# A windowed attention block with routed regions: x and the output with channels on partitions, and one reciprocal that also spreads its result

## The reference

```
xc  = group_norm(x)                                    # per image and group of 8 channels
q, k, v = split(xc @ qkv_w.T + qkv_b)                  # 256 channels each
q_r, k_r = mean of q, k over each of 7 x 7 regions     # a region is 8 x 8 positions
idx = top_k(q_r @ k_r.T, 4)                            # four regions for every region
# for every region and each of 8 heads of 32 channels:
attn = softmax((q * 256**-0.5) @ k[idx].T)             # 64 queries, 4 * 64 = 256 keys
o    = attn @ v[idx]
lepe = depthwise_conv3x3(v, lepe_w) + lepe_b
out  = x + ((o + lepe) @ out_w.T + out_b)
```

## Time and profile before

| | |
|---|---|
| median of 3 runs | 1920.2 us (1920.08 to 1926.36) |
| the profiled execution, first to last instruction | 1916.1 us |
| PE busy | 1767.0 us, 92% |
| DVE busy | 1613.2 us, 84% |
| ACT busy | 1587.6 us, 83% |
| POOL busy | 694.3 us, 36% |
| granted TensorE clock, mean | 0.990 |

### The profile page before, as it was taken

One profiled execution on the slowest core, in us unless ns is written; L12 is line 12 of the kernel. 1 busy time (PEld: TensorE's weight loads), 2 busy tenths in 40 slices (PEclk: granted clock), 3 DMA queues, 4 the chain that ended last, 5 costly groups with the idle time before them and its releaser, 6 DMA issues.

```text
span 1916.1 us, 75037 instructions
## 1 busy us (share of the span) xinstructions
PE 1767.0 (92%) x25560; PEld 1163.4 (61%) x25560; DVE 1613.2 (84%) x3819; ACT 1587.6 (83%) x5017; POOL 694.3 (36%) x2060
## 2 busy tenths in 40 slices
PE   6968999999999999999999999999999999977776
PEld 4535666666666666666666666666666666654444
DVE  4788998889998999898898899988988888876554
ACT  3648989899988999898898899888998888877775
POOL 1013433433433343434344334433433333333332
PEclk9989999999999999999999999999999999999999
DMA  4313444334443444344443344434443333333332
GB/s 114 85 48 99 113 132 113 114 112 135 118 122 99 132 119 123 110 120 117 124 115 113 109 130 118 119 109 125 116 121 97 109 97 111 103 106 90 93 101 89
DMA packets 163286, 211.71 MB, mean 110 GB/s; under 512 B 17760, under 2 KB 143840, under 8 KB 162912
## 3 DMA queue, kind: packets, MB, share of 16 engines
q1 hardware_dynamic: 141408, 129.84, 24.0%
q0 software_dynamic: 21504, 77.08, 13.3%
HBM read 155.46 MB, written 51.38 MB: 108 GB/s over the span
## 4 chain that ended last, share of the span: by engine, by line
SPq 51%; PE 25%; issue 9%; DVE 8%; DMA 5%; ACT 2%; POOL 0%; POOLq 0%; ACTq 0%; DVEq 0%
SPq L279 38%; SPq L254 11%; PE chunk_bank L818 8%; PE pt_bank L906 5%; PE s_bank L893 3%; DVE lepe L573 3%; PE o_bank L920 3%; DMA v_sel<-v_dram 3%; PE chunk_bank L836 3%; SPq L269 2%; DVE neg_max L669 1%; DMA v_dram<-v_stage 1%; ACT probs L480 1%; PE chunk_bank L851 1%; DVE stats L590 1%
## 5 line engine op out<-in xcount | busy, mean ns | idle before, releaser
L480 ACT ACTIVATE probs<-s_bank,neg_max 128x256 f32<-128x256 f32 x1568 | 735.5, 479 | 183.5 <-DVE neg_max L669 178.9
L329 POOL COPY k_sel<-k_all 128x128 f32 x1568 | 403.3, 302 | 1045.6 <-PE s_bank L893 1042.4
L573 DVE SCALAR_TENSOR_TENSOR lepe<-v_band,taps,lepe 128x448 f32<-128x448 f32 x896 | 612.9, 701 | 17.0 <-POOL v_band L345 6.0
L669 DVE TENSOR_REDUCE neg_max<-s_bank 128x2 f32<-128x512 f32 x784 | 506.3, 686 | 137.1 <-PE s_bank L893 130.3
L818 PE MATMUL chunk_bank<-xn,wqkv 128*128 128x448 f32 x1240 | 545.5, 547 | 1.0 <-DVE xn L609 0.7
L487 ACT COPY probs_t<-pt_bank 128x512 f32<-128x512 f32 x784 | 469.6, 599 | 52.4 <-PE pt_bank L906 50.9
L906 PE MATMUL pt_bank<-ident,probs 128*128 128x128 f32 x3136 | 492.6, 280 | 14.9 <-ACT probs_t L487 13.8
L906 PEld LDWEIGHTS pt_bank<-ident,probs 128*128 128x128 f32 x3136 | 359.0, 141 | 155.9 <-issue 94.7
L480 ACT ACTIVATION_READ_ACCUMULATOR probs<-s_bank,neg_max 128x1 f32 x1568 | 322.4, 206 | 0.0
L920 PEld LDWEIGHTS o_bank<-probs_t,v_sel 128*32 128x32 f32 x12544 | 194.4, 110 | 196.1 <-issue 117.3
L920 PE MATMUL o_bank<-probs_t,v_sel 128*32 128x64 f32 x12544 | 257.9, 223 | 41.2 <-DMA v_sel<-v_dram 40.3
(11 more groups left out here) (96 smaller groups left out, 1446.8 us busy)
## 6 DMA issues: line engine op xcount, KB each, us to landing
v_sel<-v_dram SPq DMA_DIRECT2D x1568, 64.0 KB
v_dram<-v_stage SPq DMA_DIRECT2D x112, 224.0 KB
x_in<-x_dram POOLq DMA_DIRECT2D x50, 448.0 KB
resid<-x_dram POOLq DMA_DIRECT2D x28, 512.0 KB, 4.8
out_dram<-resid POOLq DMA_DIRECT2D x28, 512.0 KB
resid<-x_dram POOLq DMA_DIRECT2D x28, 384.0 KB
out_dram<-resid POOLq DMA_DIRECT2D x28, 384.0 KB, 3.4
resid<-x_dram POOLq DMA_DIRECT2D x2, 448.0 KB, 7.5
```

Source lines behind the costliest of these rows:

```text
L329: last = pool.tensor_copy(k_sel[:, r % K_SLOTS, :, RT * j:RT * (j + 1)], k_all[:, b % 2, :, bass.ds(reg[j] * RT, RT)])
L480: act.activation(probs[:, u, :], s_bank[:, u, 0:KEYS], ACT.Exp, bias=neg_max[:, r % 2, u:u + 1], accum_out=denom[:, r % 2, u:u + 1]).then_ ...
L573: ins = dve.scalar_tensor_tensor(row, v_band[:, n % BANDS, k, t // 3:t // 3 + RS, t % 3:t % 3 + W], taps[:, k, t:t + 1], row, ALU.mult, AL ...
L669: dve.tensor_reduce(neg_max[:, r % 2, 2 * hf:2 * hf + 2], s_bank[:, 2 * hf:2 * hf + 2, 0:KEYS], AX.X, ALU.max, negate=True).then_inc(max_d ...
```

## The change

x is handed over with channels on partitions, [56 rows, 128 partitions, 2 halves, 448 tokens], and the output is written in the same layout. Rows of x are loaded straight into xn, which becomes a ring of 9 rows; the turning of x on PE, its copy on ACT and the staging buffers are gone. A load waits until PE has projected v and k of the row that had the place before, and DVE's moments and sums wait for the load's semaphore (`wait_x`). The output projection takes the output matrix as weights and a row of lepe as moving data, so channels are on partitions, each row has two groups of two matmuls of 448 columns, and the bias is one number a partition, which DVE adds in the same instruction as x. POOL adds no bias any more. On the softmax's side DVE's inversion of 4 sums and its spreading copy become one reciprocal, which reads each sum 32 times and writes 128 elements a partition; it waits for the sums and for the turned reciprocals of the region before. The order in which results use the PSUM banks is kept without x's entries. In the host's code x and the output are transposed.

```diff
+X_RING = NWIN + 2
...
-    x_in = sb("x_in", [TT, NT, C])
-    xn = sb("xn", [P, KC, RING, ROW])
+    xn = sb("xn", [P, KC, X_RING, ROW])
...
-    def add_bias(g, j):
-        if j == 0:
-            pool.wait_ge(resid_in[g % 2], 16 * (g // 2 + 1))
-        pool.tensor_tensor(resid[:, g % 2, j, :], resid[:, g % 2, j, :], bout[:, :],
-                           ALU.add).then_inc(resid_ready, 1)
-
     def load_x(n):
-        i, _, before = x_buffer[n]
-        if before is not None:
-            wait_full(pool, "x", before, 1)
-            wait_full(pool, "x", before, 0)
-        pool.dma_start(x_place(n), x_rows[n]).then_inc(x_loaded[i], 16)
+        if n >= X_RING:
+            for kind in ("v", "k"):
+                for k in range(KC):
+                    wait_full(pool, kind, n - X_RING, k)
+        pool.dma_start(xn[:, :, n % X_RING, :], x[n]).then_inc(x_loaded[n % X_RING], 16)
...
-    if is_row(s - 1) and rc < len(out_tiles(s - 1)):
-        add_bias(s - 1, rc)
-    if rc == 2:
-        for n in range(X_BUFFERS, ROWS):
-            if x_buffer[n][2] == s + X_LEAD:
-                load_x(n)
+    if rc == 0 and X_RING <= s + X_LEAD + 1 < ROWS:
+        load_x(s + X_LEAD + 1)
...
-    def x_out(n, k):
-        wait_full(act, "x", n, k)
-        act.copy(xn[:, k, n % RING, :], bank_of("x", n, k)[:, 0:ROW]).then_inc(free("x", n, k), 1)
...
     def x_moments(n, k):
-        wait_taken(dve, "x", n, k)
+        wait_x(dve, n)
...
     def out_half(g, m):
         if m == 0:
-            dve.wait_ge(resid_ready, PAIR_TILES * (g // 2) + out_tiles(g)[-1] + 1)
+            dve.wait_ge(resid_in[g % 2], 16 * (g // 2 + 1))
         wait_full(dve, "out", g, m)
-        n = min(2, len(out_tiles(g)) - 2 * m)
-        res = resid[:, g % 2, 2 * m:2 * m + n, :].rearrange("p j c -> p (j c)")
-        dve.tensor_tensor(res, bank_of("out", g, m)[:, 0:C * n], res, ALU.add).then_inc(free("out", g, m), 1)
+        res = resid[:, g % 2, m, :]
+        dve.scalar_tensor_tensor(res, bank_of("out", g, m)[:, 0:ROW], bout[:, m:m + 1], res, ALU.add,
+                                 ALU.add).then_inc(free("out", g, m), 1)
...
     def invert(r):
         dve.wait_ge(exp_done, HG * (r + 1))
-        dve.reciprocal(rdenom[:, r % 2, :], denom[:, r % 2, :]).then_inc(inv_done, 1)
-
-    def spread(r):
-        dve.wait_ge(inv_done, r + 1)
         if r:
             dve.wait_ge(recips_turned, r)
-        dve.tensor_copy(recips[:], rdenom[:, r % 2, :].unsqueeze(2).to_broadcast([P, HG, HD])
-                        ).then_inc(recips_done, 1)
+        dve.reciprocal(recips[:], denom[:, r % 2, :].unsqueeze(2).to_broadcast([P, HG, HD])
+                       ).then_inc(recips_done, 1)
...
-    def turn_x(n, k):
-        for j in range(NT):
-            last = pe.transpose(bank_of("x", n, k)[:, TT * j:TT * (j + 1)],
-                                x_place(n)[:, j, P * k:P * (k + 1)], ident[0:TT, 0:TT])
-        last.then_inc(full("x", n, k), 1)
...
-    def project_out(g, j):
+    def project_out(g, m, part):
...
-        for k in range(KC):
-            rows = lepe[:, k, pair:pair + 2, :].rearrange("p r t -> p (r t)")
-            ins = pe.matmul(bank_of("out", g, m)[:, C * (j % 2):C * (j % 2 + 1)], rows[:, at:at + P],
-                            wout[:, k, :], start=(k == 0), stop=(k == KC - 1))
+        ins = pe.matmul(bank_of("out", g, m)[:, 0:ROW], wout[:, part, P * m:P * (m + 1)],
+                        lepe[:, part, g % LEPE_RING, :], start=(part == 0), stop=(part == KC - 1))
```

More of the change, by code:

```diff
@@ L64, in chunk_places @@
         banks = EARLY_BANKS if s < -1 else 2
-        for key in [("x", s + X_LEAD, 0), ("v", s + A_LEAD, 0), ("out", s - 2, 1), ("v", s + A_LEAD, 1),
+        for key in [("v", s + A_LEAD, 0), ("out", s - 2, 1), ("v", s + A_LEAD, 1),
                     ("k", s + A_LEAD, 1), ("k", s + A_LEAD, 0), ("out", s - 1, 0), ("vt", s + A_LEAD, 1),
-                    ("q", s + A_LEAD + 1, 0), ("vt", s + A_LEAD, 0), ("q", s + A_LEAD + 1, 1), ("x", s + X_LEAD + 1, 1)]:
+                    ("q", s + A_LEAD + 1, 0), ("vt", s + A_LEAD, 0), ("q", s + A_LEAD + 1, 1)]:
             if 0 <= key[1] < ROWS:
@@ L124, in attention_kernel @@
         v_stage = sb("v_stage", [TWO, 4, C])
-        resid = sb("resid", [P, 2, PAIR_TILES - EVEN_TILES, C])
+        resid = sb("resid", [P, 2, KC, ROW])
         probs = sb("probs", [P, HG, KEYS])
@@ L162, in attention_kernel @@
         ident_in, weights_in, idx_in = map(sem, ("ident_in", "weights_in", "idx_in"))
-        x_loaded = [sem(f"x_loaded{i}") for i in range(X_BUFFERS)]
+        x_loaded = [sem(f"x_loaded{i}") for i in range(X_RING)]
         v_stored = sem("v_stored")
@@ L214, in free, with wait_x @@
             return chunk_free[place[kind, n, k][0]]
+        def wait_x(eng, n):
+            eng.wait_ge(x_loaded[n % X_RING], 16 * (n // X_RING + 1))
         def by_region(flat):
@@ L223, in in_image @@
             return flat.rearrange("p (r c) -> p r c", c=W)
[L225 to L242, removed]
         def is_row(n):
@@ L367, in load_resid @@
                     pool.wait_ge(out_stored[g % 2], 16 * (g // 2))
-                else:
-                    wait_full(pool, "x", NWIN - 1, 0)
-                pool.dma_start(resid_place(g), pair_tiles(resid_pairs, g)).then_inc(resid_in[g % 2], 16)
+                pool.dma_start(resid[:, g % 2, :, :], x[g]).then_inc(resid_in[g % 2], 16)
             def store_row(g):
@@ L374, in store_row @@
                 wait_taken(pool, "out", g, 1)
-                pool.dma_start(pair_tiles(out_pairs, g), resid_place(g)).then_inc(out_stored[g % 2], 16)
-            for n in range(X_BUFFERS):
+                pool.dma_start(out[g], resid[:, g % 2, :, :]).then_inc(out_stored[g % 2], 16)
+            for n in range(X_RING):
                 load_x(n)
@@ L438, in mid_tap @@
                 if n >= LEPE_RING and k == 0:
-                    before = n - LEPE_RING
-                    if before % 2 == 0:
-                        wait_full(act, "out", before + 1, 0)
-                    else:
-                        wait_full(act, "out", before, 1)
+                    wait_full(act, "out", n - LEPE_RING, 1)
                 act.activation(lepe[:, k, n % LEPE_RING, :], bank_of("v", n, k)[:, 0:ROW], ACT.Identity,
@@ L607, in normalize @@
                 dve.wait_ge(x_read, 2 * KC * (n + 1))
-                row = xn[:, k, n % RING, :]
+                row = xn[:, k, n % X_RING, :]
                 dve.tensor_scalar(row, row, rstd[:, k:k + 1], shift[:, k:k + 1], ALU.mult, ALU.add
@@ L798, in _ @@
             pe.wait_ge(ident_in, 16)
-            def turn_x(n, k):
-                if not is_row(n):
-                    return
-                i, before, _ = x_buffer[n]
-                pe.wait_ge(x_loaded[i], 16 * (before + 1))
-                wait_bank(pe, "x", n, k)
-                for j in range(NT):
-                    last = pe.transpose(bank_of("x", n, k)[:, TT * j:TT * (j + 1)],
-                                        x_place(n)[:, j, P * k:P * (k + 1)], ident[0:TT, 0:TT])
-                last.then_inc(full("x", n, k), 1)
             def project(kind, n, k, part):
@@ L970, in _ @@
                     elif rc == 4:
[L971 removed]
+                        project_out(s - 1, 0, 0)
                     if is_region(r):
```

75 lines of the change are left out of this document (18 added, 57 removed).

## The result

The changed kernel takes 1936.9 us (median of 5 runs, 1929.6 to 1938.7) where the kernel before, run beside it, takes 1921.7 (5 runs): ratio 1.0073, 95% interval 1.0053 to 1.0094. It is slower, as forecast, but by 15 us where 36 were forecast. The spans of the two profiled executions differ by 16.9 us (1933.0 against 1916.1).

A forecast was written before the change was run, and what follows sets the result against it. SP's fetches were the floor; DVE would become the bound, images lasting 229.7 us for 222.5. Span 1916.1 - 7 (start) + 6 x 7.2, plus 4.1 to the median: 1956 us, 8-in-10 range 1898 to 2010.

The forecast's parts named there:

- R: Time of the new 128-element reciprocal on DVE, once a region; taken as 0.85 us, ends 0.23 and 1.11.
- turning point: Reciprocal time from which the change loses: images pass today's 222.5 us at 0.70, the start's gain is gone at 0.73.
- pairings: Four-element reciprocals (172, 178 ns) set against two-element instructions (161, 150 ns), giving 3.2 to 7.5 ns an element.
- streaming rival: Reciprocal streams, taking up to 0.66 us, so SP's fetches set the time: 1901 us; chance 0.29.
- the serial one: Rival of fully serial division: 8 ns an element, reciprocal 1.17 us, 2060 us in all; chance 0.11.
- DVE's sum, 181.5 + 49 R: DVE's busy us an image: 199.7 now, less 19.5, plus 1.3, plus 49 new reciprocals.
- the exchange, 49 x (R - 0.397): DVE's softmax work, 49 regions an image: inversion and copy, 0.397 us together, go; one reciprocal comes.
- idle kept at 6.5 us: DVE's idle time an image that stays after the 16.3 us of waiting for scores is filled by the longer reciprocal.
- Start -7 us: Before the first regions: 3.5 us in statistics, 1.9 in PE's transposes, 1.88 in a DVE wait saved, together 7.
- SP's floor of 220.4 us: SP's value fetches limit an image without x work on PE and ACT to the seventh image's 220.4 us.
- Rival 3: SP is no floor and PE's freed 7.7 us counts in each of seven images: 1859 us; chance 0.01.
- What would show it: Signs of DVE bounding: busy above 96%, chain through DVE, holes within SP's rows, score waits gone, first store near 126.

The follow-up runs named there:

- e4: Changed kernel with reciprocals and products of 2 to 512 elements a partition added on DVE at the start; reciprocal rows grow 6.25 ns an element, fixed part 153.
- e1: Changed kernel with the inversion of 4 sums and the spreading copy put back, so the layout alone; 1923.6 us, ratio 1.0015 to the kernel before.
- e3: Changed kernel with 196 additions of the old size put back on POOL, on a tile nobody reads; 1970.7 us, ratio 1.0254.
- e2: Kernel before with the one reciprocal, so the softmax part alone; 1953.3 us, ratio 1.0170.
- e12: Changed kernel with one of four value fetches a region issued by POOL instead of SP, behind POOL's gather and edges; 1927.0 us, ratio 1.0043.
- e11: Layout alone (old inversion and copy), one of four value fetches issued by POOL instead of SP, behind POOL's gather and edges; 1844.3 us, ratio 0.9583.
- e13: Kernel before with one of four value fetches issued by POOL instead of SP, behind POOL's gather and edges; 1882.1 us, ratio 0.9802.
- e7: Changed kernel with its reciprocal over 24 of each 32 columns, 96 elements in place of 128; 1917.1 us, ratio 0.9992.
- e5: Layout alone (old inversion and copy), one of four value fetches issued by POOL instead of SP, ahead of POOL's key gather; 1902.5 us, ratio 0.9916.
- e6: Changed kernel with one of four value fetches issued by POOL instead of SP, ahead of POOL's key gather; 2008.4 us, ratio 1.0493.
- e10: Kernel before with one of four value fetches issued by POOL instead of SP, ahead of POOL's key gather; 1978.0 us, ratio 1.0303.

## Why the prediction was right in direction and wrong in size

- **R decides, and it is above the turning point**: right in kind. R is 0.945 us, inside the range of 0.23 to 1.11, 0.1 above the middle taken. The fixed part is that of the 150 to 152 ns instructions; of the pairings, 172 with 150 ns (6 ns an element) came nearest to 6.25. The streaming rival is refuted by e4; so is the serial one at 8 ns an element, with the estimate beside it that came to the same price.
- **The step that failed: DVE's sum, 181.5 + 49 R.** At the measured R it gives 227.8 us busy, measured 219.0. The term that was mis-sized most is the exchange, 49 x (R - 0.397): it took the lengths of records for time on the engine, and the exchange costs 0.41 us a region where records say 0.548, since the instructions behind the long reciprocal are shorter and more records overlap; that is 6.7 us an image. The other 2.2 us are the layout's: I had put DVE at 199.7 + 1.3 = 201.0 with the old pair, e1 has 198.8. The output addition takes 668 ns there and not the taps' 701, and the taps themselves fell to 679 without POOL's additions. I had called those 196 additions nothing, "if POOL's additions slowed DVE, a little is gained": the taps beside them in the kernel before show 2.3 us an image, and e3 shows 6.2 for additions at another place in the changed kernel.
- **The two errors hid each other**, and that the forecast is not further off is luck. R's 0.095 us more would have made the sum longer by 4.7 us an image, the failed sum made it 8.4 too long. The difference, 6 x (8.4 - 4.7) = 22 us, is about the 21 us that lie between 36 forecast and 15 measured; the last image, put at nothing, is 3.3 us longer and stands against it with smaller terms. With the right R the sum would have forecast 6 x 4.7 = 28 us more, 1984 us, further from the measured 1937.
- **The idle kept at 6.5 us**: right, 6.9 in the changed kernel, 6 to 6.9 in e2, e3 and e12, so busy time plus 6 to 7 us is what a full DVE-bound image takes here. The wait for scores was filled as said: 98 to 18.7 us.
- **Start -7 us**: right, -7.5.
- **SP's floor of 220.4 us for the layout, read from the seventh image**: wrong. The seventh is short for other reasons too, and about half of the difference is the missing transfers of x, which the layout doesn't remove. In e1 the six images stayed at 223.8 and the rival at 1901 us, priced by them, did not come even in e1, where the old pair takes 0.4 us. That SP is a floor was right (e11, e13); where it lies was not. The changed kernel's own seventh image came out near it, at 221.2, by luck: with a fetch less on SP it stays at 221.4 (e12), where the layout alone falls to 213.6 (e11). With 216 as the busy time that DVE may have, the point from which the reciprocal hurts is R near 0.87.
- **Rival 3, PE's freed time**, came out where SP is no floor: e13 to e11 is 38 us by the medians, 42 by the ratios, against the 54 + 7 of its sum. It was rightly denied for this kernel.
- **What would show it**: the chain through DVE, DVE at 97% of a full image, the wait gone and the early first store all came. Holes on SP came only at the ends of images and not within rows; SP had just 3 us an image to spare (225.9 against e7's 222.9).

## What to carry to other kernels

Price an exchange of instructions by an engine's busy time with and without it, where overlaps count once, or by the distances from start to start on a full engine, the neighbours' included; records added up overstated the long instruction that replaced two short ones. Where several engines stand within 3% of each other, a change is worth what the next bound allows: free the first one in an experiment before judging the change, as the same layout was worth 0 or 42 us, and the reciprocal on that layout cost 11 or 88. A last, lighter stage is no measure of what one kind of work costs, since several kinds end there at once.

## What the runs showed of the hardware

- DVE's reciprocal takes 153 ns and 6.25 ns an element (e4, 2 to 512 elements), where a multiplication by a constant takes 227 ns for 128.
- POOL's copies and DVE's instructions with two SBUF operands lengthen each other: a tap of 0.67 us took 1.27 beside four POOL copies, which took 394 ns on the mean for 300. Normalizing of x, with one tensor as input, grew too, the maximum from PSUM did not (e5 beside e1). The place of one DMA in POOL's order was worth 58 us on the layout alone (e5 to e11), 81 on the changed kernel (e6 to e12) and 96 on the kernel before (e10 to e13).
- The kernel that beats both, e11, has the new layout, the old pair of reciprocal and copy, and one fetch of four on POOL behind its gather: 1844.3 us.
